# Two-layer graph attention: layer-0 scores from two passes to one, sums from ScalarE, weights turned on TensorE

## The reference, cut to what matters

```python
# layer 0
q, k, v = proj(Wq, bq), proj(Wk, bk), proj(Wv, bv)          # 8 heads of 32
scores = einsum('bhqd,bhkd->bhqk', q, k) / sqrt(32)
scores = where(adj + eye > 0, scores, -inf)
out = einsum('bhqk,bhkd->bhqd', softmax(scores), v) @ Wo.T + bo
h = layernorm(x + out) * gamma + beta
# layer 1
feat = h @ fc_w.T + fc_b
logits = (feat @ q_w.T + q_b) + transpose(feat @ k_w.T + k_b) + (1 - adj) * -1e9
atten = softmax(where(logits >= 0, logits, 0.01 * logits))
return atten @ feat + h
```

## Time and profile before

| what | value |
|---|---|
| runs | 1104.35, 1094.05, 1103.16 us; median 1103.16 us |
| the profiled execution's own time | 1106.9 us |
| its span, first to last instruction | 1104.8 us |
| mean granted TensorE clock | 0.971 |
| busy share PE / PEld / DVE / ACT / POOL | 92 / 59 / 71 / 56 / 65 % |

### The profile page before, as it was taken

One profiled execution on the slowest core, in us unless ns is written; L12 is line 12 of the kernel. 1 busy time (PEld: TensorE's weight loads), 2 busy tenths in 40 slices (PEclk: granted clock), 3 DMA queues, 4 the chain that ended last, 5 costly groups with the idle time before them and its releaser, 6 DMA issues. The chain is left out here.

```text
span 1104.8 us, 16668 instructions
## 1 busy us (share of the span) xinstructions
PE 1021.8 (92%) x5720; PEld 649.2 (59%) x5720; DVE 782.6 (71%) x1945; ACT 622.8 (56%) x1180; POOL 722.8 (65%) x415
## 2 busy tenths in 40 slices
PE   5789899999999999999999998999999999999866
PEld 4445565656656565665666564666656566665454
DVE  4667777877767787777778777777767767775432
ACT  2145466565646557575655657564555746566633
POOL 3056787675667667666777766576766657778740
PEclk9899999999999999999999999999989999999978
DMA  5677827576564667667374767646366663745010
GB/s 133 106 123 145 133 73 143 102 144 96 113 116 89 135 113 144 96 121 127 102 134 83 153 115 137 103 103 119 79 141 105 136 108 99 135 76 90 29 48 28
DMA packets 81571, 120.89 MB, mean 109 GB/s; under 512 B 9296, under 2 KB 36432, under 8 KB 81488
## 3 DMA queue, kind: packets, MB, share of 16 engines
q1 hardware_dynamic: 81488, 119.84, 56.8%
HBM read 52.44 MB, written 8.39 MB: 55 GB/s over the span
## 5 line engine op out<-in xcount | busy, mean ns | idle before, releaser
L708 ACT ACTIVATE e<-st_bank 128x512 f32<-128x512 f32 x512 | 307.4, 602 | 404.1 <-PE st_bank L526 223.5
L928 DVE CUSTOM_DVE_ANT_0 sm_bank<-sm_bank,masks 128x512 f32<-128x512 f32 x512 | 354.1, 693 | 155.3 <-PE sm_bank L534 152.2
L1009 POOL TENSOR_TENSOR e_sum<-e_sum,e 128x1024 f32<-128x1024 f32 x128 | 303.7, 2385 | 49.8 <-ACT e L708 49.8
L534 PE MATMUL sm_bank<-kt_hi,q_pad 128*128 128x512 f32 x512 | 281.9, 552 | 32.9 <-issue 28.0
L524 PE MATMUL st_bank<-q_stack,k_stack 97*128 97x512 f32 x432 | 197.7, 458 | 3.8 <-ACT e L708 3.0
L1009 POOL TENSOR_TENSOR e_sum<-e 128x1024 f32<-128x1024 f32 x64 | 152.2, 2378 | 67.9 <-ACT e L708 61.1
L526 PE MATMUL st_bank<-mask_t,ident_b 128*128 128x512 bf16 x432 | 169.2, 392 | 0.0
L524 PEld LDWEIGHTS st_bank<-q_stack,k_stack 97*128 97x128 f32 x432 | 81.5, 189 | 111.5 <-ACT e L708 103.3
L462 PE MATMUL o_bank<-e,v 128*32 128x512 f32 x1024 | 136.4, 605 | 0.7 <-ACT e L708 0.7
L505 PE MATMUL shared<-feat,z 128*128 128x256 f32 x512 | 134.5, 412 | 1.4 <-ACT z L651 1.4
L534 PEld LDWEIGHTS sm_bank<-kt_hi,q_pad 128*128 128x128 f32 x512 | 103.2, 202 | 44.5 <-issue 31.8
(11 more groups left out here) (131 smaller groups left out, 1836.7 us busy)
## 6 DMA issues: line engine op xcount, KB each, us to landing
adj_in<-in_adj SPq DMA_DIRECT2D x32, 1024.0 KB, 7.8
q_stack<-qt_hi SPq DMA_DIRECT2D x64, 256.0 KB, 9.7
k_stack<-kt_hi SPq DMA_DIRECT2D x64, 256.0 KB, 8.8
x_in<-in_x SPq DMA_DIRECT2D x16, 512.0 KB, 10.4
q_pad<-qt_hi SPq DMA_DIRECT2D x128, 64.0 KB, 7.7
q_stack<-qt_lo SPq DMA_DIRECT2D x32, 256.0 KB, 8.6
k_stack<-kt_lo SPq DMA_DIRECT2D x32, 256.0 KB, 11.9
h<-in_x SPq DMA_DIRECT2D x16, 512.0 KB, 3.8
```

Of the source, the lines that this page charges most:

```text
L534: nc.tensor.matmul(sm_bank[s % 2][:, :], q_pad[j // GH][:, j % GH, qt * P:(qt + 1) * P], kt_hi[j // GH][:, :], start=True, stop=True).then ...
L708: nc.scalar.activation(e[:, kt, i, :], st_bank[s % 2][:, :], ACT.Exp, scale=SCALE)\
L928: nc.vector.tensor_tensor_reduce(sm_bank[s % 2][:, :], sm_bank[s % 2][:, :], mask[nxt if off else par][:, qt * N:(qt + 1) * N], 1.0, LOWES ...
L1009: nc.gpsimd.tensor_tensor(e_sum[:, pair, :], a, b, ALU.add).then_inc(pool_done.sem, 1)
```

## The change

The score tile is computed once, as queries x keys, from the stacked operands (now 96 rows, the query side scaled by -1/sqrt(32) already in the weights), into three banks `sm_bank` (`SCORED = 3`). VectorE adds the mask and takes the row minimum of the negated scores. ScalarE computes exp(minimum - value) with a per-partition bias and lets its accumulator give the row sum (`accum_out`). `turn` (four transposes with the identity, three positions later, `TURN = 3`) turns the unscaled exponentials on TensorE into two banks `et_bank`; 17 of the 32 turned tiles are copied to SBUF (`e_t`) by ScalarE and the 15 in `DVE_COPIED` by VectorE. `times_v` runs as four calls a batch, each with four key blocks x four heads of 256 columns. The row sums are inverted as [128, 16] (`recip_rows`), widened by GpSimd (`widen_recip`), turned (`spread_recip`), copied by ScalarE (`recips`), and multiplied in by VectorE as the output leaves PSUM (`o_normal`). Gone are the second set of score tiles, the turned mask, the pads, the placed maxima, GpSimd's sums, the ones matmul, the wide reciprocals and `normalise`. `shared` has two banks instead of three, with the bank of each step in a table. All other steps stay, but their order is new: a table for each engine (`PE_AT` and so on) gives each step a position counted from its batch's first tile.

```diff
-POS = NG * NT * GH
+TILES = NH * NT
+PAIRS = 4
-DVE_MASKED = (12, 14, 15, 26, 29)
-LEAD = 21
+TURN = 3
+ROOM = 4
+SCORED = 3
+TURNED = 2
+SHARED = 2
+DVE_COPIED = (0, 3, 5, 6, 13, 14, 15, 18, 22, 24, 25, 26, 27, 28, 29)
+PE_AT = {
+    "at3": 64, "et1": 65, "k1": 2, "rb1": 36, "pv3": 36, "at0": 69, "v1": 6, "at1": 73, "v0": 9, "xt1": -22, "op1": 44,
+    "xt0": -18, "op0": 46, "k0": -17, "q0": -16, "pv0": 17, "ht1": 50, "ht0": 50, "rb0": 21, "fc0": 53, "fc1": 54,
+    "kb": 56, "pv1": 24, "q1": -5, "pv2": 29, "et2": 62, "et3": 62, "at2": 63, "et0": 63}
+ACT_AT = {
+    "k_hi1": 2, "o_hi0": 35, "rs1": 35, "v1": 6, "o_hi1": 39, "v0": 10, "x_hi1": -22, "x_hi0": -19, "k_hi0": -17,
+    "q_hi0": -17, "hn0": 47, "hn1": 48, "h_hi1": 49, "h_hi0": 50, "rs0": 19, "feat0": 52, "feat1": 54, "logit0": 57,
+    "logit1": 57, "logit2": 57, "logit3": 58, "q_hi1": -6, "l_negmax": 59, "lexp2": 60, "lexp3": 60, "et2": 60,
+    "et3": 60, "lexp0": 61, "lexp1": 62, "et0": 63, "et1": 63}
+DVE_AT = {
+    "l_recip": 64, "rc1": 33, "fin1": 66, "k_lo1": 4, "o_n1": 38, "fin0": 73, "x_lo1": -20, "h_add1": 45, "stats1": 45,
+    "x_lo0": -18, "h_add0": 46, "stats0": 46, "moments": 46, "k_lo0": -17, "q_lo0": -16, "rc0": 18, "h_lo1": 50,
+    "h_lo0": 50, "q_dot0": 54, "q_dot1": 56, "l_max0": 56, "l_max1": 56, "o_n0": 26, "q_lo1": -4, "mask1": -1,
+    "mask0": -1}
+SP_AT = {
+    "adj": 1, "x": -30, "adj_again": 39, "stack1": 18, "store1": 85, "store0": 91, "x_again": 27, "stack0": -4}
...
+            def times_v(k, b):
+                g, half = k // 2, k % 2
...
+                for kt in range(NT):
                     for i in range(GH):
                         o = g * P + i * DH
+                        last = nc.tensor.matmul(o_bank[i * DH:(i + 1) * DH, 2 * half * P:2 * (half + 1) * P], v[:, kt, o:o + DH],
+                                                e_t[:, k % 2, kt, i, :], start=(kt == 0), stop=(kt == NT - 1))
...
+            def scores(s, b):
+                g, i, qt = tile(s)
+                if s % (TILES // NG) == 0:
+                    pe.wait_ge(stacked[g].sem, stacked[g].of(f"stack{g}", b))
+                u, earlier = ago(s, SCORED)
+                pe.wait_ge(exp_done.sem, exp_done.of(u, b + earlier))
+                nc.tensor.matmul(sm_bank[(TILES * b + s) % SCORED][:, :], q_stack[g][:, i, qt * P:(qt + 1) * P], k_stack[g][:, i, :],
+                                 start=True, stop=True).then_inc(sm_done.sem, 1)
+            def turn(u, b):
+                pe.wait_ge(exp_done.sem, exp_done.of(u, b))
+                w, earlier = ago(u, TURNED)
+                copied = dve_copied if w in DVE_COPIED else act_copied
+                pe.wait_ge(copied.sem, copied.of(w, b + earlier))
+                n = TILES * b + u
+                for c in range(NT):
+                    last = nc.tensor.transpose(et_bank[n % TURNED][:, c * P:(c + 1) * P], e[:, n % ROOM, c * P:(c + 1) * P], ident[:, :])
+                last.then_inc(turned.sem, 1)
...
+            def exponential(s, b):
+                u, earlier = ago(s, ROOM)
+                act.wait_ge(min_done.sem, min_done.of(s, b))
+                act.wait_ge(turned.sem, turned.of(u, b + earlier))
+                n = TILES * b + s
+                k, (g, i, qt) = n % ROOM, tile(s)
+                nc.scalar.activation(e[:, k, :], sm_bank[n % SCORED][:, :], ACT.Exp, scale=-1.0, bias=row_min[:, k:k + 1],
+                                     accum_out=row_sum[:, g, qt, i:i + 1]).then_inc(exp_done.sem, 1)
...
+            def o_normal(g, b):
+                dve.wait_ge(pe_done.sem, pe_done.of(f"pv{2 * g + 1}", b))
+                dve.wait_ge(act_done.sem, act_done.of(f"rs{g}", b))
+                dve.wait_ge(pool_done.sem, pool_done.of(f"o_lo{g}", b - 1))
+                nc.vector.tensor_tensor(o_raw[g][:, :], o_bank[:, :], recip_wide[g][:, :], ALU.mult).then_inc(done, 1)
...
+            def masked_minima(s, b):
...
+                nc.vector.tensor_tensor_reduce(bank[:, :], bank[:, :], mask[b % 2][:, qt * N:(qt + 1) * N], 1.0, -LOWEST,
+                                               ALU.add, ALU.min, row_min[:, k:k + 1])\
+                    .then_inc(min_done.sem, 1)
...
+            def copy_turned(u, b):
+                dve.wait_ge(turned.sem, turned.of(u, b))
+                k = u // (TILES // PAIRS)
+                dve.wait_ge(pe_done.sem, pe_done.of(f"pv{(k - 2) % PAIRS}", b - (k < 2)))
+                nc.vector.tensor_copy(turned_to(u), et_bank[(TILES * b + u) % TURNED][:, :].rearrange("p (c n) -> p c n", c=NT))\
+                    .then_inc(dve_copied.sem, 1)
```

More of the change, by code:

```diff
@@ L223, in build @@
[L223 to L224 removed]
+        shared = [pb(f"shared{i}") for i in range(SHARED)]
+        bank_of = {name: shared[n] for name, n in BANK.items()}
+        tiles = [(s, 0) for s in range(TILES)]
+        sm_done = Signal(sem("sm_done"), tiles)
+        min_done = Signal(sem("min_done"), tiles)
+        exp_done = Signal(sem("exp_done"), tiles)
@@ new lines, in build @@
+        made = {"act": act_done, "dve": dve_done}
+        loads = steps(SP_AT)
+        adj_loaded = Signal(sem("adj_loaded"), [step for step in loads if step[0] in ("adj", "adj_again")], 16)
+        x_loaded = Signal(sem("x_loaded"), [step for step in loads if step[0] == "x"], 16)
+        h_loaded = Signal(sem("h_loaded"), [step for step in loads if step[0] == "x_again"], 16)
+        stacked = [Signal(sem(f"stacked{g}"), [step for step in loads if step[0] == f"stack{g}"], 16 * 6) for g in range(NG)]
@@ L225, in build @@
+        stored = [Signal(sem(f"stored{i}"), [step for step in loads if step[0] == f"store{i}"], 16) for i in range(2)]
         weights_loaded, cols_loaded, const_loaded = sem("weights_loaded"), sem("cols_loaded"), sem("const_loaded")
@@ new lines, in attend @@
+            def attend(c, b):
+                k = c % 2
+                pe.wait_ge(act_done.sem, max(act_done.of(f"et{c}", b), act_done.all("feat", b)))
+                if k == 0:
+                    pe.wait_ge(*bank_read(f"at{c}", b))
+                bank = bank_of[f"at{c}"]
+                for kt in range(NT):
+                    last = nc.tensor.matmul(bank[:, k * D:(k + 1) * D], z[:, c, kt * P:(kt + 1) * P], feat[:, kt, :],
+                                            start=(kt == 0), stop=(kt == NT - 1))
+                last.then_inc(pe_done.sem, 1)
@@ new lines, in o_high, with recips, normal_rows @@
+            def o_high(g, b):
+                act.wait_ge(pe_done.sem, max(pe_done.of("kb", b - 1), pe_done.all("fc", b - 1)))
+                act.wait_ge(dve_done.sem, dve_done.of(f"o_n{g}", b))
+                nc.scalar.copy(o_hi[:, g, :], o_raw[g][:, :]).then_inc(act_done.sem, 1)
+            def recips(g, b):
+                copy(recip_wide[g][:, :], f"rb{g}", bank_of[f"rb{g}"][:, :], b)
+            def normal_rows(half, b):
+                act.wait_ge(pool_done.sem, pool_done.of("shift", b))
+                for c in range(2 * half, 2 * half + 2):
+                    last = nc.scalar.activation(h[b % 2][:, c, :], h[b % 2][:, c, :], ACT.Identity, bias=shift[:, c:c + 1],
+                                                scale=rstd[:, c:c + 1])
+                last.then_inc(act_done.sem, 1)
@@ new lines, in query_logits @@
+            def query_logits(half, b):
+                dve.wait_ge(act_done.sem, act_done.of(f"feat{half}", b))
+                dve.wait_ge(pe_done.sem, pe_done.all("at", b - 1))
+                for k in range(2):
+                    c = 2 * half + k
+                    last = nc.vector.tensor_tensor_reduce(z[:, c, 0:D], bank_of[f"fc{half}"][:, k * D:(k + 1) * D], qw_row[:, :],
+                                                          1.0, logit_bias[:, 3:4], ALU.mult, ALU.add, q_dot[:, c:c + 1])
+                last.then_inc(done, 1)
@@ new lines, in layer1_maxima @@
+            def layer1_maxima(half, b):
+                dve.wait_ge(dve_done.sem, dve_done.all("q_dot", b))
+                dve.wait_ge(pe_done.sem, pe_done.of("kb", b))
+                dve.wait_ge(pool_done.sem, max(pool_done.of(f"l_mask{2 * half + k}", b) for k in range(2)))
+                for k in range(2):
+                    c = 2 * half + k
+                    last = nc.vector.tensor_tensor_reduce(z[:, c, 0:N], bank_of["kb"][:, :], adj_in[:, c, :], 1.0, LOWEST,
+                                                          ALU.add, ALU.max, z[:, c, N:N + 1])
+                last.then_inc(done, 1)
```

1200 lines of the change are left out of this document (552 added, 648 removed), and 23 rows, old and new, of tables (ACT_STEPS, DVE_STEPS, PE_STEPS, POOL_AT).

## The result

The kernel after takes 985.72 us (median of 4 runs, 985.39 to 986.52); the kernel before, with a fourth run of 1099.93, has a median of 1101.55. The ratio is 0.8959, 95% interval 0.8913 to 0.9005: 10% faster. The prediction was 1032, its range 984 to 1094. The time lies 1.7 us inside the range's lower end, where rival 4 (TensorE stays dense, 984) had put it, to which I had given 8%.

A forecast was written before the change was run, and what follows sets the result against it. TensorE was taken as the bound: 55.7 of work, 4.3 of waits and 0.5 added make 60.5 us a batch. Head 43.5, tiles 938 and tail 52 sum to 1033.5; plus 2.1, less 3.7, forecast 1032, range 984 to 1094.

The forecast's parts named there:

- rival 4: TensorE stays dense, with no wait but 1.5 us a batch: P = 57.5, 984 us; chance 8%.
- P: Time of one batch in the steady part: 63.97 us in the kernel before, predicted 60.5 after.
- the tail: From the last layer-0 exponential to the end: 58.9 us before, 7 us off (2 to 11), predicted 52.
- the head: Time up to the first layer-0 exponential: 54.3 us before, predicted 43.5, bounds 39 and 50.
- The other 6.3 us of P are waits: TensorE's batch time beyond its counted work, taken as waits; 4.3 us a batch kept after the change.
- The pads: TensorE's wait for four `q_pad` DMAs at a batch's first maxima tile: about 2.0 us a batch, gone after.
- the counted 57.7: TensorE's work in a batch of the kernel before, summed from distances of starts: 57.7 us.
- 55.7: TensorE's work in a batch after the change: 55.7 us, between 55.2 and 56.8.
- 47.3 against 55.7: ScalarE's work a batch after the change, 47.3 us, claimed to hide behind TensorE's 55.7.
- Rival 1: TensorE's clock drops in light positions, two drops of 1.75 us a batch: P = 63, 1072 us; chance 12%.
- Rival 2: Adjacency matrix late for VectorE's mask at position 31, waiting 2 us a batch: P = 62.5, 1064 us; chance 8%.
- Rival 3: ScalarE decides, at positions 24 to 31, its steps waiting for other engines: P = 66.4, 1126 us; chance 12%.

The follow-up runs named there:

- e_extra: Kernel after with every score matmul issued twice into the same bank: 1098.89 us.
- b_nopad: Kernel before without its pads, the maxima matmul reading the turned q of its group: 1062.87 us, ratio 0.9679.
- b_extra: Kernel before with the maxima matmul of every tile issued twice into the same bank: 1162.03 us.
- e_bank2: Kernel after with two score banks instead of three: 1237.54 us, ratio 1.124.
- e_copies: Two runs: kernel after with 31, or 24, of its 32 copies of turned tiles a batch on ScalarE in place of 17: 1022.73 and 990.00 us.
- c_clock: Kernel after with 300 transposes, 300 matmuls and 300 transposes ahead of TensorE's program: 1107.1 us.

## Why the prediction was wrong where it was

The direction and the bound (TensorE) held, and the range by 1.7 us. The time was 46 us under the forecast. Of the span's 50.1 (1033.5 - 983.4) P makes 16 x (60.5 - 56.75) = 60, the tail 3.4, the tiles' ends -10 and the head -3.6; the remainder to 46 is the 3.7 by which I had moved the profiled execution to the median. So nearly all of it is P, and in P one step.

**The step that failed: "The other 6.3 us of P are waits", carried over as "I leave the remaining wait as it is: 6.3 - 2.0 = 4.3" with 0.5 added.** 4.8 us a batch were carried over, 77 us in all (the stream of after, 1.05 longer than summed, gave 17 of it back). In e_extra all of the added 7.4 us showed, so next to nothing of such a wait stands in after. But most of it had not been a wait in before either. What the 6.3 was, the runs now say:
- The pads: 2.0 predicted, 3.0 measured (b_nopad). The row that I used holds only the stop; the half clock behind it I counted among what stays, and in b_nopad it is gone as well.
- Waits for a score bank: some 0.7 (b_extra against b_nopad). The 103.3 us in which loads waited for exponentials look like 6.5 a batch, but a load runs ahead of its matmul, and positions whose load waited take only 0.05 us longer.
- The other 2.6: no wait, but a stream that I had summed too short. With the 0.7 it makes the 3.3 between the counted 57.7 and the 60.98 of b_nopad.

The table gives the stream in us a batch: as counted or predicted, and as the starts in the traces of b_nopad and after give it.

| part | before, counted | b_nopad | after, predicted | after |
|---|---|---|---|---|
| score tiles, masks, maxima tiles | 21.0 | 24.8 | 7.4 | 10.3 |
| turns | | | 13.4 | 12.7 |
| `times_v` | 7.9 | 8.0 | 8.4 | 7.5 |
| sums of `e` | 2.0 | 2.0 | | |
| `attend` | 7.0 | 6.3 | 7.0 | 6.4 |
| projections, key logits | 15.3 | 15.6 | 15.3 | 16.0 |
| other transposes | 4.5 | 4.3 | 4.2 | 3.9 |
| sum | 57.7 | 61.0 | 55.7 | 56.75 |

The tiles are the term that was mis-sized. I took 0.69 for a position and 0.23 for a tile from one place, between projection matmuls, where a tile costs least; behind the other steps it takes 0.32 to 0.43. The same 0.69, taken off the 2.43 between two `attend` blocks, made `attend` 1.74: it takes 1.54 there, and the position 0.89. In after the same error is 2.9 us, and `times_v` (half the columns cost half the time, with no charge for twice the instructions), the turns and `attend` took back 2.3 of it. So 55.7 was near 56.75, within its range (55.2 to 56.8), by errors that nearly cancel.

The 7.2 us a batch then are 3.0 of pads and 4.2 of the rest, of which b_extra finds 0.7 as a wait for a bank. In the table the rest is 2.0 for the sums that ScalarE's accumulator now gives, about 1.7 for a tile and its turn in place of tile, mask and maxima tile, 0.5 for `times_v`, and little else. The prediction had 2.0 for all of the stream. The third bank brings little by itself in these numbers; it keeps the merged pass from waiting (e_bank2).

**ScalarE.** The exponential was priced at 0.69 from start to start with its sum; it takes 0.68 (299.76 to 300.44):

```profile
299.76 0.69 ACT L679 ACTIVATE e<-sm_bank,row_min 128x512 f32<-128x512 f32 x1
300.34 0.20 ACT L679 ACTIVATION_READ_ACCUMULATOR e<-sm_bank,row_min 128x1 f32 x1
300.44 1.95 ACT L606 ACTIVATE z<-z,q_dot 128x513 f32<-128x513 f32 x3
```

It stayed hidden, as predicted, though with less room than the 47.3 against 55.7 suggests: the e_copies runs put the edge between 50.7 and 54.

**The head** was 47.1, predicted 43.5. The pads were no cost in SyncE's queue. The first and the last of its six stack issues in after, then what its queue waited for:

```profile
31.00 0.66 SPq L298 DMA_DIRECT2D q_stack<-qt_hi  x1
...
34.30 0.61 SPq L299 DMA_DIRECT2D k_stack<-kt_lo  x1
```
```profile
SPq L295 <- DVE qt_lo L842: 16.9, 1, 16.9
```

SyncE stood for 16.9 us waiting for VectorE's low part of the queries; what sets the stacks is that, and in before the four pads had been issued in such a wait: b_nopad, without them, issued its last stack at 33.92, later than before's 32.60. So the last issue came at 34.30, not at 30.1, and 34.3 plus 11.1 of landing plus 1.7 for tile and minimum is 47.1.

**The tail** was 48.6, predicted 52. Up to the last output projection it took as predicted: 943.7 - 934.8 = 8.9 against 9.1.

```profile
943.69 0.47 PE L388 MATMUL shared<-weight_hi,split_hi 128*128 128x256 f32 x1
```

The part behind it, which I had taken as unchanged, was 3 us shorter (39.7 against 42.8). No run looked into why.

**The rivals.** Rival 1 (clock) did not happen: 1.00 over the steady part, and c_clock shows that turns count like other work. Rival 2: VectorE waited for no `adj_in` in the steady part. Rival 3 did not happen either, but e_bank2 shows that it is real and far dearer than my 1126: with one bank fewer it takes 1238. I had its argument for (a tile passed on four times) and the argument against it (three banks), and the second was worth 16 us a batch. Rival 4 is the one whose mechanism came true, TensorE dense, but that its 984 lies within 2 us of the time is luck: its P of 57.5 is 0.75 too high (12 us), the tiles at both ends, the head and the tail together took 10 us more than the sum has for them, and the other 3.7 are what it took off for the median. 8% was too little: when a forecast says that an engine is the bound, a dense engine is the default, and a wait that stays needs a reason of its own.

What stays open: what a third score bank would bring in before (b_extra finds 0.7, and no run tried it), the last 0.3 of the pads' 3.0, and why a tile costs more behind some steps than behind others.

## What to carry to other kernels

What is left when counted work is taken off measured time is not yet a wait. Price each instruction between the neighbours that it has, at more than one place, before calling the rest a wait and carrying it over; then ask of each wait whether the change removes what it waits for. A buffer that two consumers hold in turn may need a copy more than buffers held by one each: here two banks in place of three cost 16 us a batch. To look for slack, double an instruction of known length in front of the wait, and then read in that run's trace which wait has gone: the 3.7 that b_extra hid were mostly the pads' time, which another run had already counted.

## What the hardware did that I had not expected

- What a fast 512-column matmul costs depends on what ran before it: the score tile of after takes 0.23 us behind a projection matmul, 0.32 behind transposes, 0.34 behind `times_v` and 0.43 behind `attend`. The first tile of a position in b_nopad takes the same four times.
- Half as many columns in twice the instructions cost nothing extra: 16 groups of eight 256-column `times_v` matmuls at 0.47 us each, where eight 512-column ones took 0.99.
- Transposes alone bring TensorE to full speed (0.2 us each in the first 4 us, then 0.11) and hold the clock at 1.00 (300 in 32.8 us).
- A turn of four transposes out of the fast fp32 type takes 0.32 us on the mean in place of 0.40, not half.
- A weight load's wait need not delay TensorE: in b_nopad positions whose load had waited 0.79 us for an exponential took 0.05 us longer than the others.
- One short stop of TensorE a batch cost 3.0 us where its own rows show 2.0; with it went the half-clock stretches of the steady part (mean 0.99 to 1.00).
